# A gated state-space block with a quantized feed-forward part on one core: another order of the feed-forward steps, and GpSimd makes three roundings of tokens and two of down tiles

## What is computed

```python
# 4 batches, 256 tokens, 256 channels; context [4, 256, 128]
x = x + tanh(g_xattn) * ssm(ctx, z=layernorm(x))
x = x + tanh(g_ffn)   * ffn(layernorm(x))

# ssm: u = silu(conv(in_proj @ ctx)), DS = 16 states per channel
delta = softplus(dt_proj @ dt_lo + bias)
state = state * exp(delta * A) + (delta * u) * B_t     # a scan over 256 tokens
y = (sum over states of state * C_t + D * u) * silu(z)

# ffn, hidden size 1024, weights rounded to -1, 0, 1
act_quant(x) = clip(round(x * 128 / absmax), -128, 127), per token
inter = silu(act_quant(x) @ w_gate) * (act_quant(x) @ w_up)
out   = act_quant(hadamard(inter)) @ w_down            # fwht over 1024
```

## Time and profile before

| what | us |
|---|---|
| median of 3 runs | 265.46 (264.85 to 266.59) |
| the profiled execution | 265.58 |
| its span, first to last instruction | 263.8 |

### The profile page before, as it was taken

How to read it: one execution, slowest core, us unless ns; L and a number is a source line. 1 busy time by engine, 2 the same in 40 slices (tenths; PEclk the granted TensorE clock), 3 DMA queues, 4 the chain that set the end, 5 groups by cost and what they waited for, 6 DMA issues and landing times. The chain is left out here.

```text
span 263.8 us, 3694 instructions
## 1 busy us (share of the span) xinstructions
PE 187.3 (71%) x1209; PEld 155.8 (59%) x1216; DVE 213.9 (81%) x340; ACT 157.3 (60%) x271; POOL 147.5 (56%) x213
## 2 busy tenths in 40 slices
PE   3779489895595569867667787675596768474945
PEld 2547388794494468647557666564485547342944
DVE  4489997898989499579989897998959775579872
ACT  1685996949234556994776799735748504650040
POOL 1100890999961096039999942999930399008500
PEclk9999855899779559999997999999979988989597
DMA  3891000000000000000000000000000000000001
GB/s 60 268 363 75 1 4 0 0 1 2 0 0 2 0 0 1 2 1 0 0 2 0 0 20 4 20 4 0 0 0 24 0 20 2 0 0 1 20 22 40
DMA packets 8149, 6.34 MB, mean 24 GB/s; under 512 B 2202, under 2 KB 7874, under 8 KB 8130
## 3 DMA queue, kind: packets, MB, share of 16 engines
q1 hardware_dynamic: 7154, 6.02, 7.1%
q10 hardware_dynamic: 976, 0.09, 0.3%
HBM read 5.05 MB, written 1.05 MB: 23 GB/s over the span
## 5 line engine op out<-in xcount | busy, mean ns | idle before, releaser
L1105 POOL TENSOR_SCALAR driveT<-duT,BT 128x256 f32<-128x256 f32 x120 | 62.2, 538 | 41.0 <-issue 21.3
L823 ACT ACTIVATE decay<-delta,zero_c,aneg 128x255 f32<-128x255 f32 x128 | 65.2, 589 | 1.7 <-DVE delta L1254 1.6
L1230 DVE TENSOR_TENSOR_SCAN state<-decay,BC 128x512 f32<-128x512 f32 x30 | 36.4, 1213 | 4.4 <-issue 4.3
L1272 DVE TENSOR_TENSOR prod<-state,BC 128x1024 f32<-128x1024 f32 x32 | 38.5, 1204 | 0.6 <-issue 0.6
L463 PE MATMUL PY<-id,prod 128*128 128x128 f32 x256 | 37.9, 297 | 1.4 <-DVE x L1294 1.0
L1230 DVE TENSOR_TENSOR_SCAN state<-decay,UP 128x512 f32<-128x512 f32 x30 | 35.8, 1193 | 0.0
L463 PEld LDWEIGHTS PY<-id,prod 128*128 128x128 f32 x256 | 32.8, 154 | 2.5 <-issue 1.2
L447 PE MATMUL BC<-bc,sel 96*128 96x256 bf16 x64 | 13.1, 288 | 27.4 <-DVE prod L1272 27.3
L1130 POOL TENSOR_TENSOR wnat<-wnat 128x512 f32<-128x512 f32 x18 | 22.9, 1274 | 15.9 <-DVE wnat L1352 15.2
L933 ACT COPY hT<-GP 128x1024 f32<-128x1024 f32 x8 | 8.1, 1010 | 35.0 <-PE GP L612 35.0
L407 PE MATMUL BC<-id,driveT 128*128 128x128 f32 x120 | 21.2, 305 | 10.9 <-POOL driveT L1105 10.8
(11 more groups left out here) (208 smaller groups left out, 412.7 us busy)
## 6 DMA issues: line engine op xcount, KB each, us to landing
wnat<-in_L_ffn_w_gate_dram SPq DMA_DIRECT2D x1, 1024.0 KB, 9.6
xs<-in_x_dram SPq DMA_DIRECT2D x1, 1024.0 KB, 12.0
wnat<-in_L_ffn_w_up_dram SPq DMA_DIRECT2D x1, 1024.0 KB, 11.5
wnat<-in_L_ffn_w_down_dram SPq DMA_DIRECT2D x1, 1024.0 KB, 11.3
out_dram<-ot SPq DMA_DIRECT2D x8, 128.0 KB, 1.7
ctxs<-in_ctx_dram SPq DMA_DIRECT2D x1, 384.0 KB, 7.1
ctxs<-in_ctx_dram SPq DMA_DIRECT2D x1, 128.0 KB, 2.8
inw<-n_L_xattn_in_proj_w_dram SPq DMA_DIRECT2D x1, 128.0 KB, 2.6
```

Of the source, the lines that this page charges most:

```text
L823: last = nc.scalar.activation(decay[:, m % RING, h, n, 1:L], delta[:, b % 2, h, 1:L], ACT.Exp, bias=zero_c[:], scale=aneg[:, h, NB * j + n ...
L1105: last = nc.gpsimd.tensor_scalar(driveT[:, m % RING, c, n], duT[:, b % 2, c], BT[:, b % 2, c, NB * j + n:NB * j + n + 1], 1.0, ALU.mult, A ...
L1230: nc.vector.tensor_tensor_scan(state[:, g % STATES, h].rearrange("p n l -> p (n l)"), decay[:, g % RING, h].rearrange("p n l -> p (n l)"), ...
L1272: nc.vector.tensor_tensor(prod[:, g % RING].rearrange("p h n l -> p h (n l)"), state[:, g % STATES].rearrange("p h n l -> p h (n l)"), PC. ...
```

## The change

The main loop of every list is put in another order. In the notation above:

- PE: `gate(f, 0)` and `up(f, 0)` both at s = 3, then `gate(f, 1)` and `up(f, 1)` both at s = 4, after `q2_T(p, 1)` and ahead of the next step's `drive_rows`. `gate(f, 1)` now waits for the DVE product of tile 0. `x_dbl(n)` moves from s = 6 to s = 5, `in_proj` of batch 3 to s = 1 and 2. `inter_T(f, 0)` moves from s = 7 to 6, `hadamard_mm(f, 0)` from s = 0 of the next batch to s = 7 of this one. `hadamard_mm(p, 1)` goes ahead of `C_rows` at s = 2, `q2_T(p, 0)` to s = 1.
- DVE: `absmax2(p, 0)` at s = 0 instead of 1, `absmax2(p, 1)` at the head of s = 3, `gate_times_up` after the product of s = 4 and 5 instead of ahead of that of s = 5 and 6. `round_tokens` and `round_down(p, 1)` leave its loop.
- POOL: `drives(g + 5)` instead of `drives(g + 4)`; the whole softplus tail at s = 1 and 2; `weight_scale(1)` and `(2)` ahead of the drives of s = 3; the roundings of the tokens at the head of s = 3 and of the second down tile at the head of s = 4; the folds one step earlier.
- ACT: `rstd2(f)` and `quant_down(p, 0)` at s = 0, after the decays, `rstd2` ahead of `softplus`; `copy_duT` at s = 3 ahead of the table load; `q2_out_early(p, 1)` between the two silus; the copies of x_dbl after the decays of s = 7.
- Three PSUM banks of the front and their waits change: duT of batch 2 goes to a bank of `GP`, silu(z) of batch 1 to `UP`, and the transform of tile 0 of batch 2 to `GP`.
- Tail: `absmax2(2, 0)` is the first thing on DVE, `hadamard_mm(2, 1)` and `q2_T(2, 0)` are ahead of `tokens_T(3)` on PE.

The semaphores `dve_q` and `dve_q2` are called `rounded` and `rounded_down` now. The core of the diff:

```diff
+LEAD = 5
...
             def gate(f, t):
...
                 elif f < B - 1:
-                    pe.wait_ge(act_sg, LC * f + 1)
+                    pe.wait_ge(dve_mul, LC * f + 1)
...
             def up(f, t):
...
-                if f == B - 1:
-                    pe.wait_ge(act_sg, LC * f + t + 1)
-                elif t == 0:
-                    pe.wait_ge(act_sg, LC * f + 2)
-                else:
-                    pe.wait_ge(dve_mul, LC * f + 1)
+                pe.wait_ge(act_sg, LC * f + t + 1)
...
+            def round_tokens_early(f):
+                pool.wait_ge(act_xr, f + 1)
+                nc.gpsimd.tensor_scalar(q[:], xn[:], MAGIC + QB - 1, MAGIC, ALU.min, ALU.subtract).then_inc(rounded, 1)
+
+            def round_down_early(f, t):
+                pool.wait_ge(act_tq, LC * f + t + 1)
+                nc.gpsimd.tensor_scalar(q2[:, t], tq, MAGIC + QB - 1, MAGIC, ALU.min, ALU.subtract).then_inc(rounded_down, 1)
...
+                    if s == 3:
+                        if k == 0:
+                            weight_scale(1)
+                            weight_scale(2)
+                    if s == 3:
+                        if new:
+                            round_tokens_early(f)
+                    if s == 4:
+                        if old:
+                            round_down_early(p, 1)
+                    if g + LEAD < B * STEPS:
+                        drives(g + LEAD)
...
                     if s == 0:
+                        if old:
+                            quant_down(p, 0)
+                        if new:
+                            rstd2(f)
                         if 1 <= k < B - 1:
                             softplus(k + 1)
...
                     if s == 3:
-                        if new:
-                            round_tokens(f)
-                    if s == 4:
-                        if old:
-                            round_down(p, 1)
+                        if old:
+                            absmax2(p, 1)
...
                     times_C(g)
...
+                    if s == 4:
+                        if new:
+                            gate_times_up(f, 0)
+                    if s == 5:
+                        if new:
+                            gate_times_up(f, 1)
```

More of the change, by code:

```diff
@@ L1020, in _ @@
                         if new:
-                            rstd2(f)
-                        if old:
-                            quant_down(p, 0)
-                        if new:
                             second_norm(f)
@@ L1459, in _ @@
                             split(1)
-                    if s == 2:
                         if old:
```

177 lines of the change are left out of this document (77 added, 100 removed).

## The result

The changed kernel takes 273.97 us in the median of four runs (272.01 to 279.82), the kernel before 266.02 beside it: ratio 1.027, interval 1.017 to 1.037. The forecast of 262.7 and its range are missed, on the slow side. The profiled execution took 272.01 us with a span of 270.2, 6.4 above that of before.

The account below looks back on a forecast made before the run. DVE was taken to set the pace in the loop, busy 213.9 of 263.8 us. The batch and tail terms sum to -5.0, the clock adds 2.1: 265.58 - 5.0 + 2.1 = 262.7 us, range 258.5 to 267.5.

Parts of the forecast that it names:

- Batch 0, -3.0: First batch: earlier weight scaling frees DVE's second rounding (-1.7), earlier x_dbl removes a scan wait (-1.3); 3.0 us saved.
- the bound of 0: Batch 0: no gain if DVE's hold only moves to the next pair of instructions; the other end was -3.5.
- Batch 1, -2.1: Batch k = 1: the 3.52 us wait for rstd2 goes, first gate-times-up starts at 109.0, not 113.35; net 2.1 us saved.
- the one named as weakest: Batch 1: the POOL instructions ahead of the token rounding, called least sure, +-0.7.
- Batch 2, +1.0: Batch k = 2: DVE's waits rise from 4.0 to 7.0 us while its work falls by 2.0; 1.0 us longer.
- Batch 3, -1.1: Batch k = 3: idle time 7.0 against 6.3, with 1.1 and 0.8 off DVE's work; 1.1 us saved.
- Tail, +0.2: Tail: an absmax and a Hadamard product go ahead of the residual, others leave the tokens' way; 0.2 us longer.
- The bound of +3: Tail: the slow end, depending on PE's clock at the two Hadamard products; the other end was -1.5.
- Clock, +2.1: PE in k = 1, 2, 3: new idle times bring more half-clock stretches, costing 2.1 us; ends 0 and 7.
- One and a half stretches: Count of extra low-clock stretches on PE, each 2.8 us long and losing 1.4 us of PE work.
- the head of PE's queue decides: Rival: 4.3 us of PE work between up 0 and up 1 takes 8.6 at half clock; 269.2 us, chance 0.14.
- a small risk: Rival that GpSimd, busy 38.0 of 46.9 in k = 2 and given 1.7 more, becomes the bound; held inside 265.1.

Follow-up runs that it names:

- e3: Kernel before with only the batch 0 edits (weight scalings earlier, five drives ahead, x_dbl of batch 2 one step earlier): 265.54 us, ratio 0.999.
- e19: Changed kernel with absmax2(p, 0) and its quantization, rounding and transposes one step later: 268.39 us, ratio 1.016 to the kernel before.
- e6: Changed kernel with extra transposes of a constant on PE in two idle times of k = 2 and 3: 276.21 us, ratio 1.045 to the kernel before.
- e11: Kernel before with serial gate and up, and the duT copy moved ahead of ACT's silus: 264.47 us, ratio 0.998.
- e13: Changed kernel with the tail, first Hadamard product, its absmax and followers, and shared gate and up of the kernel before: 262.83 us.
- e14: Changed kernel with the old tail and the first absmax and followers one step later, Hadamard product still early: 264.56 us, ratio 0.994 to kernel before.
- e7: Changed kernel with the tail order of the kernel before on all engines: 272.93 us, four runs, 268.1 to 274.6.
- e17: Changed kernel with absmax2(p, 0) and its followers one step later and the roundings back on DVE: 266.33 us, ratio 1.005 to the kernel before.

## Why the prediction was wrong

- *Batch 0, -3.0.* The profile says -3.2, but that was luck: 1.7 over all profiles, and 0.2 in the median of e3 alone. The second weight rounding came at 2.13, as written; in e3 it was 2.60 and the wait moved to the first one, which is the bound of 0. The step that failed is taking a shorter batch 0 for a shorter kernel.
- *Batch 1, -2.1.* It was -0.3. The wait at `rstd2`'s reader is gone, as said. The step that failed is not the one named as weakest, the instructions ahead of the rounding, but the rounding itself: put at 0.62 by the nearest row it takes 1.93, and the two-input operation at 1.27, the upper end, was no bound. The scan at 94.08 waits 1.76 as well. The first gate-times-up starts 27.9 behind the first product of batch 1 instead of the 26.3 foreseen (109.0 - 82.7).
- *Batch 2, +1.0.* It was +6.3. DVE's work fell by 2.1 (2.0 foreseen). Its waits: 1.88 (1.55), 3.00 (0.7), 2.19 and 2.36 (3.4), 2.69 (0.9), 12.1 instead of 6.6. The wait at the head of the list, "`absmax2(0, 0)` at s = 0 ... Wait 1.55", was sized well. The step that failed is the sum behind it: the three later places were worked out at the full clock and as if dt_proj, the tokens and PE's queue were on time, 5.0 in all, and they took 10.2. The stand is a wait, with 1.7 of work, ahead of the product, the residual and the split. I didn't ask, of this added wait, who waits for what is queued behind it: PE's accumulation (2.16) and dt_proj (3.12), and through dt_proj the softplus and the tokens. Nor did I ask what the transposes `q2_T(0, 0)` and ACT's quantization, one step earlier, stand ahead of. 13.7 us at the lower clock followed in the same queue. With the absmax and its followers back (e19) the later waits are 6.8 and none stands at s = 0; which of the two carries how much is open.
- *Batch 3, -1.1.* It was +1.8; the same stand is there (1.88 at 177.48), and in e19, without it, the batch takes 45.4, as in the kernel before.
- *Tail, +0.2.* It was +2.3, and 3.3 over all profiles (50.0 in six with the new tail, 46.7 in fourteen with the old). The same pattern: `absmax2(2, 0)` goes ahead of the residual and waits 5.69, since its Hadamard product is queued behind two accumulations, the transposes of tile 1 and D*u; the kernel before waits 3.36 at that point and has the residual done at 221.3. The bound of +3 was nearly right, the value not.
- *Clock, +2.1.* "One and a half stretches" of 2.8 us was the term furthest off: one stretch lasted 13.7. The count is near (five in batches 1 to 3, three before), the length is not: in k = 1 of the kernel before stood one of 12.9, and I took the short one of k = 2. An estimate from the clock column of the stretches: PE was at the lower clock for 42 us of batches 1 to 3, and for 21 in the kernel before; the forecast had 4 more. How much of the loss the clock makes by itself stays open: e6 shows only that it doesn't make dt_proj start late, and no run changed the clock alone.
- *The rivals.* The one that ended slower, "the head of PE's queue decides", had the sign and the clock, but another place: not between up 0 and up 1, but at the start of the batch. By e11 and e13 the serial order costs between nothing and 2.7. GpSimd's roundings: 2 of the loss, more than "a small risk".

By the runs: taking the absmax and its followers one step back is worth 5.6 in the changed kernel (e19), and 8.4 with the old tail (e14 against e7). The old tail is worth 3.8 with them back (e14 against e19) and 1.0 alone (e7, four runs). Both together come to 264.56, already 0.7 under the kernel before. In what remains of the change, GpSimd's roundings cost 2.1 (e17) and the serial order 2.7 by e13; e11 has it at 0, but together with the early copy of duT, which may pay for it. Against them stand the early r, that copy and batch 0. Each of these is a difference of medians, good to about 1 us at best, and they don't add exactly.

## What to carry to other kernels

Of an instruction that is put ahead of another on an in-order engine, price not only its own wait but what the readers of everything behind it lose: here an absmax that waited 1.9 us ahead of a product and a split, with what follows it one step early on ACT and PE, made the batch 5 us longer. A part that alone reproduces a loss is not thereby its cause in the whole; the test is to take it out of the whole. And a batch that gets shorter in one profile is a gain only when the median says so.

## What was not expected of the hardware

- GpSimd's `tensor_scalar` with min and subtract takes 1.93 us for 128x512 and 3.62 for 128x1024, multiply-add on the same shapes 0.6 and 1.04. DVE does the rounding in 0.43 and 0.69. The Trainium skill (GPSIMD Engine Reference, section 4.1) has GpSimd about as fast as the Vector engine with one input; the multiply-add comes near it, the rounding does not, by a factor of four to five.
- A small operation of DVE, the split's last one (32x256), takes 0.60 in the changed kernel, 1.08 in e19 and 2.95 in e6, each time with GpSimd busy beside it. Since dt_proj waits for it, this alone moves dt_proj by over 2 us; what it depends on wasn't tried.
- Feeding PE in its idle times did not keep its clock up at the places that mattered (e6): the low stretch began 14 us behind the start of batch 2 instead of 7 and still lasted 10, and the time rose by 2.2. The Trainium skill (TensorE: Matmul & The Clock Gate, Part 1) puts an idle PE at half its clock, and the changed kernel's stretch at 127.0 begins right behind an idle time of 2.16 us; but in e19 an idle time of 1.66 passed without one (its low stretch begins at 134.1, behind 3.47).
